# Two self-attention layers on a 32x32 image: scores kept with the keys on the partitions, and a softmax shift sent across partitions

## What is computed

```python
xn = group_norm(x, gamma, beta)                    # 32 groups, eps 1e-5 / 1e-6
q = conv1x1(xn, wq, bq).reshape(B, N, C)           # N = 1024, C = 256
k = conv1x1(xn, wk, bk).reshape(B, N, C)
v = conv1x1(xn, wv, bv).reshape(B, N, C)
scores = jnp.einsum('bnc,bmc->bnm', q, k) * scale
attn = jax.nn.softmax(scores, axis=-1)
out = jnp.einsum('bnm,bmc->bnc', attn, v).reshape(B, H, W, C)
return conv1x1(out, wp, bp) + x
```

## Time and profile before

| what | value |
|---|---|
| median of 3 runs | 291.37 us |
| lowest, highest | 290.06, 291.91 us |
| span of the profiled execution | 289.3 us |
| around the span, to the median | 2.1 us |
| TensorE busy (matmul) | 278.0 us |
| VectorE busy | 194.1 us |
| ScalarE busy | 125.2 us |
| GpSimd busy | 53.7 us |

### The profile page before, as it was taken

One profiled execution on the slowest core, in us unless ns is written; L12 is line 12 of the kernel. 1 busy time (PEld: TensorE's weight loads), 2 busy tenths in 40 slices (PEclk: granted clock), 3 DMA queues, 4 the chain that ended last, 5 costly groups with the idle time before them and its releaser, 6 DMA issues.

```text
span 289.3 us, 5131 instructions
## 1 busy us (share of the span) xinstructions
PE 278.0 (96%) x1586; PEld 239.7 (83%) x1586; DVE 194.1 (67%) x457; ACT 125.2 (43%) x239; POOL 53.7 (19%) x123
## 2 busy tenths in 40 slices
PE   3999999999999999999999999999999999999995
PEld 2887998788888898788888898788888898888884
DVE  1499779855576688865567688966558476556562
ACT  3467453433364564343344574334334355333340
POOL 2020204111400204111400204211300113111100
PEclk9999999999999999999999999999999999999999
DMA  5950000000000000000000000010001000000011
GB/s 163 343 185 3 0 3 0 0 0 0 1 1 0 0 0 0 0 0 0 0 0 0 0 0 0 0 36 18 18 18 39 18 0 2 18 18 18 18 36 36
DMA packets 5952, 7.19 MB, mean 25 GB/s; under 512 B 556, under 2 KB 4664, under 8 KB 5944
## 3 DMA queue, kind: packets, MB, share of 16 engines
q1 hardware_dynamic: 5920, 7.08, 7.4%
q10 hardware_dynamic: 24, 0.01, 0.1%
HBM read 4.99 MB, written 2.10 MB: 25 GB/s over the span
## 4 chain that ended last, share of the span: by engine, by line
PE 80%; DVE 12%; issue 3%; DMA 2%; DVEq 1%; SPq 0%; POOL 0%
PE S L809 25%; PE O L851 16%; PE T L681 10%; PE O L852 8%; PE T L844 7%; PE O L681 4%; PE X L851 3%; DVE neg_max L593 2%; DVE xn L538 2%; DMA xnat<-in_x 2%; PE X L681 2%; PE X L732 2%; DVE pT_lo L607 1%; PE X L852 1%; PE S L732 1%
## 5 line engine op out<-in xcount | busy, mean ns | idle before, releaser
L851 PE MATMUL O<-V,pT_hi 128*128 128x512 f32 x224 | 82.2, 405 | 0.8 <-DVE xnat L623 0.8
L406 ACT CAST pT_hi<-T 128x512 fp32r<-128x512 f32 x64 | 34.4, 590 | 88.8 <-PE T L844 88.8
L852 PE MATMUL O<-V,pT_lo 128*128 128x256 f32 x224 | 62.9, 281 | 0.0
L593 DVE TENSOR_REDUCE neg_max<-S 128x1 f32<-128x1024 f32 x32 | 39.1, 1222 | 32.6 <-PE S L809 32.6
L851 PEld LDWEIGHTS O<-V,pT_hi 128*128 128x128 f32 x224 | 42.1, 188 | 10.6 <-issue 1.5
L400 ACT ACTIVATE probs<-S,exp_bias 128x1024 f32<-128x1024 f32 x32 | 35.8, 1118 | 22.0 <-DVE exp_bias L601 21.9
L852 PEld LDWEIGHTS O<-V,pT_lo 128*128 128x128 f32 x224 | 42.3, 189 | 0.0
L607 DVE TENSOR_TENSOR pT_lo<-T,pT_hi 128x512 fp32r<-128x512 f32 x64 | 41.1, 683 | 0.2 <-issue 0.2
L309 POOL TENSOR_TENSOR xnat<-xnat,out_bias (+2 forms) x32 | 23.6, 739 | 66.9 <-DVE t_lo L631 66.9
L844 PE MATMUL T<-ident,probs 128*128 128x128 f32 x256 | 33.4, 273 | 1.2 <-ACT probs L400 1.2
L844 PEld LDWEIGHTS T<-ident,probs 128*128 128x128 f32 x256 | 29.6, 142 | 5.5 <-DVE pT_lo L607 2.5
(11 more groups left out here) (143 smaller groups left out, 433.6 us busy)
## 6 DMA issues: line engine op xcount, KB each, us to landing
xnat<-in_x SPq DMA_DIRECT2D x8, 256.0 KB, 7.0
out<-xnat SPq DMA_DIRECT2D x16, 128.0 KB, 1.9
wide<-in_vectors SPq DMA_DIRECT2D x2, 384.0 KB, 7.6
w_wq<-in_L_conv_wq SPq DMA_DIRECT2D x2, 256.0 KB, 5.0
w_wk<-in_L_conv_wk SPq DMA_DIRECT2D x2, 256.0 KB, 5.1
w_wv<-in_L_conv_wv SPq DMA_DIRECT2D x2, 256.0 KB, 6.9
w_wp<-in_L_conv_wp SPq DMA_DIRECT2D x1, 256.0 KB, 6.8
w_wp<-in_L_conv_wo SPq DMA_DIRECT2D x1, 256.0 KB, 7.2
```

The source lines that it names most:

```text
L406: nc.scalar.copy(pT_hi[:, parity, h * BPH:(h + 1) * BPH, :], PT[h][:, :].rearrange("p (m n) -> p m n", m=BPH)).then_inc(ac_pT, 1)
L593: nc.vector.tensor_reduce(neg_max[:, parity:parity + 1], S[parity][:], AX_X, ALU.max, negate=True).then_inc(dv_max, 1)
L851: nc.tensor.matmul(bank[:], pT_hi[:, parity, m, :], V[:, m, :], start=(m == 0), stop=False)
L852: last = nc.tensor.matmul(bank[:, C:2 * C], pT_lo[:, parity, m, :], V[:, m, 0:C], start=False, stop=(m == NB - 1))
```

## The change

- **Layout.** A unit's queries go in two chunks of 512. `scores(c, kb)` makes one tile of 128 keys (partitions) by 512 queries; eight tiles make a chunk. So the exponentials come out with the keys on the partitions, as attention needs them, and the eight transposes of each query row are gone.
- **Maximum.** ScalarE copies each score tile from PSUM to SBUF (`score_copy`). VectorE keeps a running maximum R of a chunk's tiles. Four transposes of R (`maxima_by_query`), a reduce, and the two bias operations (`query_shift`) give each query's negated maximum; four more transposes send it to all partitions (`shift_to_all`), ScalarE copies it to M (`maxima`).
- **Shift and exponentials.** GpSimd adds M to every tile in SBUF (`shifted`; the last chunk's odd tiles go to VectorE). ScalarE makes two exponentials of each tile, one rounded to fp32r (`P_hi`), one in fp32, and VectorE's `p_low` takes their difference, both inputs in SBUF. The sum over keys is a column of ones in V.
- **Order on TensorE.** t of the first half, values, scores of the unit's first chunk, attention of the chunk before it (the previous unit's second), t of the second half, scores of the second chunk, attention of the first. The maxima and the shift of the chunk that follows stand in the middle of an attention; in unit 0, whose first chunk has no attention before it, after the second t product and behind score tile 0. The last chunk's attention takes tile after tile into the four ring banks.
- **Banks.** t, values and scores take turns in a ring of four one-bank buffers; two banks hold attention, X the transposes of maxima and shifts, Z the next unit's rows and statistics.
- **Attention** has three matmuls a tile (258, 256, 258 columns) where it had two (512, 256); `output` has one wide operation where it had two.
- The next unit's rows are transposed straight from the input rows, without ScalarE's copy `xstat`; `normalise` works in place. A and the constants are addressed by layer, without GpSimd's copies. `residual` runs eight in a row at the start of a unit.
- All loops are unrolled.

The core of the diff (the head stage only takes other banks):

```diff
+    RING = 4
+    TILES = 12
...
+    ring_order = []
+    for u in range(UNITS):
+        ring_order += [("t", u, 0, k) for k in range(KC)]
+        ring_order += [("V", u, m) for m in range(NB)]
+        ring_order += [("S", 2 * u, kb) for kb in range(NB)]
+        ring_order += [("t", u, 1, k) for k in range(KC)]
+        ring_order += [("S", 2 * u + 1, kb) for kb in range(NB)]
+    ring_place = {tile: n for n, tile in enumerate(ring_order)}
...
+            def residual(u, i):
+
+                pool.wait_ge(pe_xT, u * NR + i // 2 + 1)
+                rows = xnat[:, u % IMAGES, i, :]
+                nc.gpsimd.tensor_tensor(rows, rows, out_bias[:, u // IMAGES, :], ALU.add).then_inc(po_resid, 1)
+
+            def shifted(c, kb):
+                pool.wait_ge(ac_M, c + 1)
+                tile = S[:, tile_of(c, kb), :]
+                nc.gpsimd.tensor_tensor(tile, tile, M[:], ALU.add).then_inc(po_D, 1)
...
+            pool.wait_ge(dv_ob, 1)
+
+            for u in range(UNITS):
+                for i in range(NB):
+                    residual(u, i)
+                for kb in range(NB):
+                    shifted(2 * u, kb)
+                    if u < UNITS - 1 and kb == (4 if u == 0 else NB - 1):
+                        power(u + 1)
+                for kb in range(NB):
+                    if not shifted_by_vector(2 * u + 1, kb):
+                        shifted(2 * u + 1, kb)
...
+            def score_copy(c, kb):
+
+                if c * NB + kb >= TILES:
+                    act.wait_ge(dv_P, c * NB + kb - TILES + 1)
+                act.wait_ge(pe_S, c * NB + kb + 1)
+                nc.scalar.copy(S[:, tile_of(c, kb), :], bank_of("S", c, kb)[:]).then_inc(ac_S, 1)
+
+            def maxima(c):
+
+                if c:
+                    act.wait_ge(*count_D(c - 1, NB - 1))
+                act.wait_ge(pe_M, c + 1)
+                nc.scalar.copy(M[:], X[:]).then_inc(ac_M, 1)
+
+            def exponentials(c, kb):
+                if c * NB + kb >= TILES:
+                    act.wait_ge(pe_O, ((c * NB + kb - TILES) // NB + 1) * QB)
+                act.wait_ge(*count_D(c, kb))
+                tile = tile_of(c, kb)
+                nc.scalar.activation(P_hi[:, tile, :], S[:, tile, :], ACT.Exp)
+                nc.scalar.activation(S[:, tile, :], S[:, tile, :], ACT.Exp).then_inc(ac_P, 1)
...
+                for kb in range(NB):
+                    score_copy(second, kb)
+                    if kb == 0:
+                        if more:
+                            raw_rows(u + 1, 3, Z)
+                        if not u:
+                            maxima(first)
+                    elif u and kb in (1, 2, 4, 5):
+                        exponentials(first, {1: 4, 2: 5, 4: 6, 5: 7}[kb])
+                    elif not u:
+                        exponentials(first, kb - 1)
+                if not u:
+                    exponentials(first, NB - 1)
+
+                if more:
+                    for q in range(TQ):
+                        xn_high(u + 1, q)
+                maxima(second)
+                for kb in range(3):
+                    exponentials(second, kb)
+            for kb in range(3, NB):
+                exponentials(CHUNKS - 1, kb)
...
-
-                dve.wait_ge(dv_max, u * NB + i + 1)
-                w = w_row[:, bass.ds(i, 1)]
-                nc.vector.scalar_tensor_tensor(exp_bias[:, parity:parity + 1], neg_max[:, parity:parity + 1], w, w,
-                                               ALU.subtract, ALU.add).then_inc(dv_bias, 1)
...
-                                            PT[h][:, :].rearrange("p (m n) -> p m n", m=BPH),
-                                            pT_hi[:, parity, h * BPH:(h + 1) * BPH, :].bitcast(F32),
-                                            ALU.subtract).then_inc(dv_pT, 1)
...
+            def running_max(c, kb):
+                dve.wait_ge(ac_S, c * NB + kb + 1)
+                if kb > 1:
+                    dve.wait_ge(dv_R, count_R(c, kb - 1))
+                earlier = R[:] if kb > 1 else S[:, tile_of(c, 0), :]
+                nc.vector.tensor_tensor(R[:], earlier, S[:, tile_of(c, kb), :], ALU.max).then_inc(dv_R, 1)
...
+
+                dve.wait_ge(pe_R, c + 1)
+                nc.vector.tensor_reduce(neg_max[:], X[:, :].rearrange("p (j n) -> p j n", j=QB), AX_X, ALU.max,
+                                        negate=True).then_inc(dv_max, 1)
+                dve.wait_ge(dv_V, (c // 2 + 1) * NB)
+                w = w_row[:, (c % 2) * QB:(c % 2 + 1) * QB]
+                dve.wait_ge(dv_max, c + 1)
+                nc.vector.tensor_tensor(neg_less[:], neg_max[:], w, ALU.subtract).then_inc(dv_shift, 1)
+                dve.wait_ge(dv_shift, 2 * c + 1)
+                nc.vector.tensor_tensor(neg_shift[:], neg_less[:], w, ALU.add).then_inc(dv_shift, 1)
+
...
+            def p_low(c, kb):
+                dve.wait_ge(ac_P, c * NB + kb + 1)
+                tile = tile_of(c, kb)
+                nc.vector.tensor_tensor(P_lo[:, tile, :], S[:, tile, :], P_hi[:, tile, :].bitcast(F32), ALU.subtract
+                                        ).then_inc(dv_P, 1)
+
+            def output(c, j, bank):
+                n = c * QB + j
+                inv = row_inv[:, n % 2:n % 2 + 1]
+                dve.wait_ge(pe_O, n + 1)
+                nc.vector.reciprocal(inv, bank[:, C:C + 1]).then_inc(dv_inv, 1)
+                dve.wait_ge(po_resid, n + 1)
+                dve.wait_ge(dv_inv, n + 1)
+                rows = xnat[:, (c // 2) % IMAGES, (c % 2) * QB + j, :]
+                nc.vector.scalar_tensor_tensor(rows, bank[:, 0:C], inv, rows, ALU.mult, ALU.add).then_inc(dv_O, 1)
...
+                if u:
+                    output(before, 0, O[0])
+                    query_shift(first)
+                    output(before, 1, O[1])
+                    p_low(first, 0)
+                    output(before, 2, O[0])
+                    p_low(first, 1)
+                    if more:
+                        statistics_of(u + 1, 2)
+                    output(before, 3, O[1])
+                    p_low(first, 2)
+                for k in range(KC):
+                    t_low(u, 1, k)
+                if u:
+                    p_low(first, 3)
+                else:
+                    query_shift(first)
+                    statistics_of(u + 1, 2)
+
+                for kb in range(1, NB):
+                    running_max(second, kb)
+                    if kb == 1 and more:
+                        statistics_of(u + 1, 3)
+                        channel_statistics(u + 1)
+                    if u and kb in (1, 2, 4, 5):
+                        p_low(first, {1: 4, 2: 5, 4: 6, 5: 7}[kb])
+                    if not u and kb > 1:
+                        p_low(first, kb - 2)
+                    if more and kb == 3:
+                        group_deviation(u + 1)
+                    if more and kb == 5:
+                        variance(u + 1)
+                if more:
                     affine_map(u + 1)
                     normalise(u + 1)
-                with dve.Fori(0, NB // 2 - 1) as j:
-                    for k in range(2):
-                        i = 2 * j + k
-                        row_max(u, i + 2, k)
-                        bias_of(u, i + 2, k)
-                        p_low(u, i + 1, 1 - k)
-                        output(u, i, k, O)
-                p_low(u, NB - 1, 1)
-                if not last:
+                if not u:
+                    p_low(first, NB - 2)
+                    p_low(first, NB - 1)
+
+                output(first, 0, O[0])
+                query_shift(second)
+                if more:
                     xn_low(u + 1, 0)
-                output(u, NB - 2, 0, X)
-                if not last:
                     xn_low(u + 1, 1)
-                output(u, NB - 1, 1, O)
-
-            with dve.Fori(0, UNITS - 1) as u:
-                unit(u, False)
-            unit(UNITS - 1, True)
+                output(first, 1, O[1])
+                if more:
+                    xn_low(u + 1, 2)
+                    xn_low(u + 1, 3)
+                else:
+                    shifted(second, 1)
+                    shifted(second, 3)
+                p_low(second, 0)
+                output(first, 2, O[0])
+                if not more:
+                    shifted(second, 5)
+                    shifted(second, 7)
+                p_low(second, 1)
+                output(first, 3, O[1])
+                p_low(second, 2)
+            for kb in range(3, NB):
+                p_low(CHUNKS - 1, kb)
+            for j in range(QB):
+                output(CHUNKS - 1, j, ring[j])
...
+            def scores(c, kb):
+                u, h = divmod(c, 2)
+                pe.wait_ge(dv_t, u * TQ + (h + 1) * KC)
+                wait_for_bank("S", c, kb)
+                bank = bank_of("S", c, kb)
+                keys = slice(kb * P, (kb + 1) * P)
+                cols = slice(h * BANK, (h + 1) * BANK)
```

(95 more changed lines are left out.)

618 lines of the change are left out of this document (260 added, 358 removed).

## The result

The changed kernel takes 308.9 us (median of 4 runs, 308.1 to 309.7) against 291.5 for the kernel before in the same series: it is slower by 17.4 us, 6.0% by the medians. The ratio on record, which goes by the fast runs alone, is 1.0625, with a 95% interval of 1.0599 to 1.0651. Forecast was 315, so the sign held, and the sum was 6 us too high.

What follows compares the result with a forecast made beforehand. TensorE, busy 96%, bounds the kernel before. Without waits the last matmul would end at 262.1 us; 45.5 of waits make 307.6, the tail a span of 313.1, and 2.1 around it 315 us; range 298 to 326.

Steps and rivals of the forecast that it cites:

- Unit 0: Waits of 20.7 us, 16.7 of them TensorE's stall before its first attention, 2.0 the restart at a low clock.
- the tail: After the last matmul: 3.0 us to the end of four outputs in a row, 2.5 for the store, 5.5 together.
- values at the unit's start: Fifth values tile waits 2.3 us for its bank, as GpSimd's last shifts and VectorE's low parts take turns.
- shift, attention of 2nd chunk: Mid attention, output, reduce and small steps take 2.5 us against 1.9 of cover: a wait of 0.6.
- second t product open: Scores follow the second t product at once and want both t tiles: 1.7 us open in each unit.
- mean and variance: Statistics stand behind VectorE's running maxima: TensorE waits 1.3 us for the mean and 0.8 for the variance.
- shift behind normalising: First chunk's attention, units 1 and 2: shift behind affine map, normalise and output 0, ready at 5.5, wanted at 3.4: 2.1 us.
- The turns: VectorE operations with two SBUF inputs and GpSimd instructions reading SBUF block each other; whichever starts first holds the ports.
- rival (b): No turns for 512-wide operations: waits of 32.7 us, time 302 us; chance 0.25.
- (c): The forecast itself: VectorE and GpSimd take turns, waits of 45.5 us, time 315 us; chance 0.45.
- Rival (d): GpSimd's next add always wins over a waiting VectorE, so residual adds hold p_low and v_low too: 326 us; chance 0.15.
- Rival (a): Queues run ahead of plan, TensorE stays the bound, only open t steps are left: 276 us, faster; chance 0.08.

Runs made afterwards that it cites:

- the run with the extra matmuls: Changed kernel plus 36 useless 512-column matmuls in unit 0 before TensorE's wait for the last P_lo: 306.6 us.
- The memset of equal length: Changed kernel with GpSimd's shift adds replaced by memsets of 1,392 columns that read nothing, shift left out of the exponentials: 300.6 us.
- the run with the shift first: Changed kernel with output 0 and the second chunk's query shift ahead of affine map and normalise in units 1 and 2: 319.4 us.
- the last experiment: Earlier reorderings and four VectorE adds kept; query shift put before each attention's first output, P_lo 3 and 4 behind values 3 and 7: 283.5 us.
- the run with the power last: Changed kernel with GpSimd's power for unit 1's variance after all eight adds of chunk 0 instead of after five: 308.8 us.

## Why the prediction was right

**The ends of the stages** show it term by term. The first t matmul of each unit after, from the timeline:

```profile
23.08 0.59 PE L841 MATMUL ring<-xn_hi,A_lo 128*128 128x512 f32 x1
...
92.25 0.39 PE L841 MATMUL ring<-xn_hi,A_lo 128*128 128x512 f32 x1
...
160.25 0.39 PE L841 MATMUL ring<-xn_hi,A_lo 128*128 128x512 f32 x1
...
228.26 0.40 PE L841 MATMUL ring<-xn_hi,A_lo 128*128 128x512 f32 x1
```

Unit 0 takes 69.2 us and units 1 and 2 take 68.0 each. The forecast's sums (11.7 is an attention, four times 2.92), with unit 0 holding one attention fewer (60.2 - 11.7 + 20.7 = 69.2, and 60.2 + 8.8 = 69.0), said 69.2 and 69.0. From 228.26 to the last matmul at 303.08 and 0.3 for its end it is 75.1; forecast 77.1. The rest from there to the span's end is 4.0; forecast 5.5. So of the 6 us too many, 2.0 are in units 1 and 2, 2.0 in unit 3, 1.5 in the tail, and none in unit 0.

**TensorE's own work** (262.1 with no wait) was right: its attention has 24 matmuls in 2.9 us and a unit without its waits comes to 60.4 (68.0 less the 7.6 below).

**Unit 0** came to the right sum by errors that cancel, which is luck. The attention starts 25.5 us after the shift transposes (52.31 to 77.81), forecast 26.7: GpSimd's wait for the variance, the late adds, and low parts behind the normalising are all in the trace. The values took 1.7 us over their work instead of 0.7. The low clock costs 1.7 us at the attention, by the run with the extra matmuls, against a forecast of 2.0; a second fall at 58, which I did not foresee, lies inside the stall. What the stall consists of I had only half right: moving the power took nothing from it, and the variance had to move as well.

**Units 1 and 2,** by stages of unit 1, each less its own matmuls:

```
                              forecast   measured
values at the unit's start      2.3        1.5
shift, attention of 2nd chunk   0.6        0.3
second t product open           1.7        1.8
mean and variance               2.1        2.4
shift behind normalising        2.1        1.6
sum                             8.8        7.6
```

The mis-sized terms are the unit's start and the two shifts. Unit 3 has the start 0.9 us below its forecast too, each of its two shifts 0.3 below, and the last chunk 1.4 instead of 2.0. At the start the forecast let p_low(3) wait for GpSimd's last add and end at 7.5 us into the unit; it ended at 6.5 (98.77), because t_low(1) was done at 4.9 (97.14) and not at 5.9: an add and a low part paired at 1.5 to 1.8 us, not at the 1.9 of 1.27 + 0.64. Mean, variance and the t product held within 0.3, and the runs that moved them got back what was charged: 4.5 us of two units' mean and variance in the trace, 4.9 by the medians (forecast 4.2), and 5.4 of three t products in the trace, 6.2 by the medians (5.1).

**The tail** was mis-sized: four outputs from PSUM pace at 0.66 us each (302.60, 303.26, 303.92, 304.58), so that the last ends 1.7 us behind the last matmul, where I had laid out 3.0.

**The turns** were the right mechanism and rival (b) is refuted as the state of this kernel: P_lo's 0.96 and the add's 1.52 are its rows. Their price was too high. Between (b) and (c) I had 13 us: 5.1 in unit 0, 1.9 at each of three unit starts and 2.0 in the last chunk. The memset of equal length gives 8.3: 3.7 in unit 0, 0.7 in each of units 1 and 2, and 2.6 in unit 3 with the last chunk. The Trainium skill's SBUF — State Buffer (Who interferes with whom) has a two-input VectorE operation blocked by a GpSimd instruction that reads SBUF and not by one that only writes; the traces agree: P_lo took 0.71 in the mean with the memsets and 0.96 with the adds. It also counts a single-input `tensor_scalar` in its two-port mode among the operations that block, which I passed over: in the run with the shift first the four normalising steps took 4.84 us beside the adds, and 1.92 without them. That they ran in that mode no row shows. Rival (d) fell at the unit's start: the residual adds began at 98.26, when p_low(3) was nearly done, and the one low part beside them (100.60) took 0.78 us against 0.69. Rival (a), all queues ahead of plan, failed in every unit; but the last experiment comes within 8 us of its 276, by order and four adds on VectorE. The "some 7" us of small waits taken away don't follow from the forecast's other numbers: its last matmul at 307.6 against 285.7 before leaves 45.5 - 18.4 - 21.9 = 5.2. Nothing in the sum uses them.

## What to carry to other kernels

When a change takes work off the bounding engine, ask what each remaining hand-over will wait for in the queue of the engine that feeds it: here 18 us of TensorE work went and about 41 us of waits came (20.7, twice 7.6, and 5.2 at the end), those that are listed all released by VectorE and 8 us of them the price of its turns with GpSimd, though VectorE was never more than 72% busy. Move steps one at a time and look for what they now run beside: a shift made 1.4 us earlier cost 10.5, and a product moved ahead of 2.9 us of other work gave all of its latency back. And measure a wait by the stage it stands in, from first matmul to first matmul, since the listed idle time leaves part of it out.

## What the runs showed of the hardware

- Turns hit operations of two elements as hard as those of 512: 0.97 and 1.18 us instead of 0.16 beside a row of adds (the run with the power last), while P_lo's 512 columns took 1.78 instead of 0.69.
- The four normalising steps, with one wide SBUF input each, stretch beside GpSimd's adds as well: 4.84 us against 1.92.
- One memset on GpSimd took 0.96 us for 1,024 columns and 1.26 for 1,392, and left P_lo at 0.69 and 0.71 in the mean.
- The granted clock fell behind a wait of 2.4 us (0.60 from 58 in the kernel after), so a stall much shorter than the 9.8 us one was enough. Where that wait was 1.3 us (the run with the power last) it was still 1.00 from 58 on, and fell behind the next one, of 4.8.
